# A two-layer decoder on one core: the order of all pieces on every engine set anew, in all five stages at once

## The reference, cut to what matters

```
x = x + bitnet_attention(ln(x), w_q, w_k, w_v, w_o)   # 16 heads of 16, causal; ternary weights, 8-bit activations
x = x + wkv(w, u, k=ln(x), v=ctx)                      # a recurrence over the 128 tokens, per channel
x = x + bitlinear(sigmoid(x1) * x2, w3)                # x1, x2 = bitlinear(ln(x), w1 / w2), ternary, width 704
x = x + attention(rope(q), rope(k), v) @ Wo            # 32 heads of 8 channels, 8 key heads, no mask
x = x + attend(q, [ssm_k, k], [ssm_v, v]) @ Wo         # q of [ctx, ln(x)]; keys of ctx in a window of 64,
                                                       # of ln(x) in one of 32; causal, with ALiBi
x = x + ln(x) @ W_base + b + shared low rank + top 2 of 6 low-rank experts
```

## Time and profile before

| what | us |
|---|---|
| median of three runs | 776.13 |
| lowest, highest | 775.43, 779.71 |
| the profiled execution, its whole time | 773.48 |
| its span in the trace | 771.7 |

### The profile page before, as it was taken

The page is one execution under the profiler, slowest core; times in us unless marked ns, Lnnn a source line. Parts: engine busy times, 40 slices in busy tenths (PEclk is TensorE's granted clock), DMA queues, the critical chain, the costliest instruction groups (busy, mean ns, idle before and its releaser), DMA issues. The chain is left out here.

```text
span 771.7 us, 19045 instructions
## 1 busy us (share of the span) xinstructions
PE 645.9 (84%) x6669; PEld 359.8 (47%) x6692; DVE 572.1 (74%) x1632; ACT 507.1 (66%) x1229; POOL 297.1 (39%) x472
## 2 busy tenths in 40 slices
PE   1598998865668779889999986799999999998885
...
DVE  5588886679999997678778754567676666666786
ACT  3588888587768766468887763366666766665421
...
GB/s 161 141 163 125 162 176 67 60 35 58 36 44 37 35 21 35 36 90 83 73 71 77 84 34 91 61 56 87 68 56 88 69 72 79 53 46 11 35 28 42
DMA packets 162303, 54.90 MB, mean 71 GB/s; under 512 B 148448, under 2 KB 160160, under 8 KB 161952
## 3 DMA queue, kind: packets, MB, share of 16 engines
...
## 5 line engine op out<-in xcount | busy, mean ns | idle before, releaser
L1163 DVE TENSOR_REDUCE l1x_neg_max<-bank 128x2 f16<-128x448 f32 (+1 forms) x192 | 119.6, 641 | 47.6 <-PE bank L1270 44.8
L1218 ACT ACTIVATE l1x_probs<-bank 128x512 f32<-128x512 f32 x192 | 106.4, 595 | 54.6 <-PE bank L1291 40.5
L871 DVE TENSOR_REDUCE l1a_neg_max<-bank 128x4 f16<-128x512 f32 x128 | 83.5, 684 | 32.7 <-PE bank L959 32.0
L1115 POOL TENSOR_TENSOR q_stack<-l1x_q_sum,q_stack 128x512 f16<-128x512 f32 x16 | 18.5, 1157 | 183.8 <-ACT q_stack L1210 183.8
L919 ACT ACTIVATE l1a_probs<-bank 128x512 f32<-128x512 f32 x128 | 69.5, 595 | 27.6 <-PE bank L973 27.0
L1662 PE MATMUL bank<-mix_xT_parts,w_ternary 128*128 128x256 f16 x384 | 50.0, 283 | 6.1 <-DVE mix_hidden L1544 4.0
L558 DVE TENSOR_REDUCE l_neg_max<-bank 128x4 f16<-128x512 f32 x64 | 42.3, 683 | 13.6 <-PE bank L685 13.6
L1662 PEld LDWEIGHTS bank<-mix_xT_parts,w_ternary 128*128 128x128 f16 x384 | 37.8, 102 | 15.3 <-DVE mix_hidden L1544 6.4
L1475 POOL TENSOR_TENSOR mix_hidden_parts<-mix_hidden,mix_hidden_parts 128x256 f16<-128x256 f32 x48 | 38.0, 804 | 15.1 <-ACT mix_hidden_parts L1607 15.1
L631 ACT ACTIVATE l_probs<-bank 128x512 f32<-128x512 f32 x64 | 36.6, 599 | 10.7 <-PE bank L705 10.7
L1734 POOL TENSOR_TENSOR moe_rstd<-moe_var_eps,minus_half 128x1 f32<-128x1 f32 x16 | 8.8, 550 | 75.2 <-DVE moe_var_eps L1752 75.2
...
## 6 DMA issues: line engine op xcount, KB each, us to landing
...
```

The lines of the kernel that those rows point to most:

```text
L871: dve.tensor_reduce(mm[:, 16 * j + 4 * s:16 * j + 4 * s + 4], b_s[c % 3][:].rearrange("p (r k) -> p r k", k=P), AX.X, ALU.max, negate=True ...
L1163: dve.tensor_reduce(mm[:, first:first + count], scores, AX.X, ALU.max, negate=True).then_inc(s_max, 1)
L1218: act.activation(prob[:, c, :], b_st[c % 2][:], ACT.Exp).then_inc(s_exp, 1)
```

## The change

Every entry of `ORDERS`, `PACE` and `TIMES` is replaced, and `clock` takes four paces a stage, one for each quarter of its batches, in place of one. No instruction is added or removed, and no semaphore, buffer or piece is changed.

```diff
 ORDERS = {
     ("l0", "dve"): order("""
-        S.2 F1+4 T3b-3 S.3 F1b+4 T3c-3 F3b+3 F8b.0+2 F3c+3 T3s-3 F3d+3 F1c+4 F8b.1+2 F8s+3 T5-3 S.0+1 S.1+1 T1-2
-        T1b-2 T3-2"""),
+        F3d T3s-6 F8b.0-1 F8b.1-1 T5-6 F1+2 F8s S.0-2 T1-5 S.1-2 T1b-5 T3-5 F1b+2 T3b-5 T3c-5 S.2-2 S.3-2 F3b+1 F3c+1
+        F1c+2"""),
     ("l0", "act"): order("""
-        F5+2 OE-2 ST.2-1 ST.3-1 F3+3 F8a.0+2 F8a.1+2 T3d-3 M T3e-3 F3e+3 T4-3 ST.0 F3f+3 F8v+2 ST.1"""),
+        T4-6 F3f ST.0-3 ST.1-3 F5 F3+1 OE-4 ST.2-3 ST.3-3 T3d-5 T3e-5 F8a.0 F8a.1 M-2 F3e+1 F8v"""),
     ("l0", "pe"): order("""
-        T4-3 S.0+1 T5-3 F5+3 T1-2 ST.1 S.1+1 F7+3 PV M+1 ST.0+1"""),
+        T4-6 M-3 ST.0-3 T5-6 F5 S.0-2 T1-5 ST.1-3 S.1-2 F7 PV-3"""),
...
     ("l1a", "act"): order("""
-        ST.7-2 ST.0-1 ST.1-1 F5+3 F8a.0+2 F8a.1+2 ST.2-1 ST.3-1 OE.1-2 M T4-3 ST.4-1 ST.5-1 F8+3 OE.0-1 ST.6-1"""),
+        ST.5-5 OE.0-5 ST.6-5 ST.7-5 F5 ST.0-4 ST.1-4 F8a.0-1 OE.1-5 ST.2-4 F8a.1-1 ST.3-4 T4-6 M-3 F8 ST.4-4"""),
     ("l1a", "pe"): order("""
-        T1.0-3 S.2 ST.0-1 PV.1-2 T1.1-3 S.3 ST.1-1 F7+3 T4-3 M ST.2-1 PV.0-1 S.0+1 T5-3 ST.3-1 S.1+1 F5+4"""),
+        ST.0-4 PV.1-5 T1.1-6 S.3-3 ST.1-4 F7 T4-6 M-3 S.0-2 ST.2-4 PV.0-4 T5-6 ST.3-4 S.1-2 F5+1 T1.0-5 S.2-2"""),
     ("l1x", "sp"): order("""
-        G-2 X-1 M-3 V-3"""),
+        X V-2 M-2 G"""),
...
     ("l1x", "act"): order("""
-        ST.0-1 ST.1-1 V+1 OE.1-2 F5+2 ST.2-1 ST.3-1 F8a.0+2 ST.4-1 ST.5-1 T4-2 F8a.1+2 ST.6-1 M ST.7-1 ST.8-1
-        ST.9-1 OE.0-1 ST.10-1 ST.11-1"""),
+        V-1 OE.1-4 F5 ST.2-3 ST.3-3 F8a.0 ST.4-3 ST.5-3 T4-4 ST.6-3 ST.7-3 M-2 ST.8-3 ST.9-3 F8a.1 OE.0-3 ST.10-3
+        ST.11-3 ST.0-2 ST.1-2"""),
     ("l1x", "pe"): order("""
-        ST.0-1 PV.1-2 S.3 ST.1-1 F5+2 S.4 T1.1-2 F7+2 ST.2-1 S.5 T4-2 ST.3-1 M T5-2 S.0+1 ST.4-1 PV.0-1 S.1+1
-        ST.5-1 T1.0-1 S.2+1"""),
+        S.4-2 T1.1-4 F7 ST.2-3 S.5-2 T4-4 ST.3-3 T5-4 M-2 S.0-1 ST.4-3 PV.0-3 ST.5-3 S.1-1 T1.0-3 ST.0-2 S.2-1 PV.1-3
+        S.3-1 ST.1-2 F5+1"""),
...
     ("moe", "pe"): order("""
-        DOWN-1 LORA-2 TR UP-2"""),
+        DOWN-1 LORA-2 UP-2 TR+1"""),
 }
...
-PACE = {"l0": (0, 8, 8.0, 11.73), "mix": (150.0, 1.35, 15.88, 5.97), "l1a": (263.0, 1.53, 8.18, 15.58), "l1x": (441.5, 6.93, 13.05, 26.37), "moe": (677.0, 5.96, 4.55, 4)}
+PACE = {"l0": (0, 1.941, (6.473, 6.712, 10.692, 8.665), 10.545),
+        "mix": (141.42, 2.413, (19.619, 5.266, 26.628, 11.892), 4.987),
+        "l1a": (248.9, 2.09, (8.933, 5.156, 7.122, 10.398), 13.65),
+        "l1x": (411.09, 11.822, (16.158, 18.43, 8.739, 9.691), 24.684),
+        "moe": (648.04, 7.98, (4.321, 5.181, 2.717, 13.573), 5.015)}
...
-    start, fill, pace, drain = PACE[stage]
-    return start + fill * min(turn - 1, 0) + pace * min(max(turn - 1, 0), n - 1) + drain * max(turn - n, 0)
+    start, fill, paces, drain = PACE[stage]
+    part = (n - 1) / len(paces)
+    run = sum(pace * min(max(turn - 1 - k * part, 0), part) for k, pace in enumerate(paces))
+    return start + fill * min(turn - 1, 0) + run + drain * max(turn - n, 0)
```

More of the change, by code:

```diff
@@ L128 @@
     ("l1a", "pool"): order("""
-        R+2 Rb+2 F1c+4 V+1 F8b+2"""),
+        R-1 Rb-1 V-2 F1c+1 F8b-1"""),
     ("l1a", "dve"): order("""
-        F1c+3 S.2-1 S.3-1 T1.0-4 F1+4 T1b.0-4 S.4-1 S.5-1 T1.1-4 S.6-1 T1b.1-4 S.7-1 F3+3 F1b+4 S.0 S.1 T5-4"""),
+        S.2-3 F1c+1 T1.0-6 F1+2 T1b.0-6 S.3-3 S.4-3 S.5-3 T1.1-6 T1b.1-6 S.6-3 S.7-3 F3+1 S.0-2 F1b+2 S.1-2 T5-6"""),
     ("l1a", "act"): order("""
-        ST.7-2 ST.0-1 ST.1-1 F5+3 F8a.0+2 F8a.1+2 ST.2-1 ST.3-1 OE.1-2 M T4-3 ST.4-1 ST.5-1 F8+3 OE.0-1 ST.6-1"""),
+        ST.5-5 OE.0-5 ST.6-5 ST.7-5 F5 ST.0-4 ST.1-4 F8a.0-1 OE.1-5 ST.2-4 F8a.1-1 ST.3-4 T4-6 M-3 F8 ST.4-4"""),
@@ L134 @@
     ("l1a", "pe"): order("""
-        T1.0-3 S.2 ST.0-1 PV.1-2 T1.1-3 S.3 ST.1-1 F7+3 T4-3 M ST.2-1 PV.0-1 S.0+1 T5-3 ST.3-1 S.1+1 F5+4"""),
+        ST.0-4 PV.1-5 T1.1-6 S.3-3 ST.1-4 F7 T4-6 M-3 S.0-2 ST.2-4 PV.0-4 T5-6 ST.3-4 S.1-2 F5+1 T1.0-5 S.2-2"""),
     ("l1x", "sp"): order("""
-        G-2 X-1 M-3 V-3"""),
+        X V-2 M-2 G"""),
     ("l1x", "pool"): order("""
-        F8b+3 F1c+4"""),
+        F1c+1 F8b"""),
     ("l1x", "dve"): order("""
-        S.2 F1+3 S.3 S.4 F1b+3 T1.0-2 F3+2 S.5 S.6 T1b.0-2 S.7 S.8 T1.1-2 T1b.1-2 S.9 F8+2 S.10 S.11 F1c+3 T5-2
@@ L142 @@
-        S.0+1 S.1+1 F8b+2"""),
+        S.7-2 S.8-2 T1.1-4 T1b.1-4 S.9-2 F1+1 S.10-2 S.11-2 F1b+1 F1c+1 F8 T5-4 F3+1 S.0-1 F8b S.1-1 S.2-1 S.3-1
+        T1.0-3 S.4-1 S.5-1 T1b.0-3 S.6-1"""),
     ("l1x", "act"): order("""
-        ST.0-1 ST.1-1 V+1 OE.1-2 F5+2 ST.2-1 ST.3-1 F8a.0+2 ST.4-1 ST.5-1 T4-2 F8a.1+2 ST.6-1 M ST.7-1 ST.8-1
-        ST.9-1 OE.0-1 ST.10-1 ST.11-1"""),
+        V-1 OE.1-4 F5 ST.2-3 ST.3-3 F8a.0 ST.4-3 ST.5-3 T4-4 ST.6-3 ST.7-3 M-2 ST.8-3 ST.9-3 F8a.1 OE.0-3 ST.10-3
+        ST.11-3 ST.0-2 ST.1-2"""),
@@ L146 @@
     ("l1x", "pe"): order("""
-        ST.0-1 PV.1-2 S.3 ST.1-1 F5+2 S.4 T1.1-2 F7+2 ST.2-1 S.5 T4-2 ST.3-1 M T5-2 S.0+1 ST.4-1 PV.0-1 S.1+1
-        ST.5-1 T1.0-1 S.2+1"""),
+        S.4-2 T1.1-4 F7 ST.2-3 S.5-2 T4-4 ST.3-3 T5-4 M-2 S.0-1 ST.4-3 PV.0-3 ST.5-3 S.1-1 T1.0-3 ST.0-2 S.2-1 PV.1-3
+        S.3-1 ST.1-2 F5+1"""),
     ("moe", "sp"): order("""
-        UP-2"""),
+        UP-6"""),
     ("moe", "pool"): order("""
-        LNc+2"""),
+        LNc+4"""),
     ("moe", "dve"): order("""
-        GATEg-2 LORA-2 LNc+1 LN+2 LOGIT-1 LOGITb-1 XN+1 GATE-1 GATEb-1 UP-2 GATEc-1 GATEd-1 GATEe-1
@@ L155 @@
-        GATEf-1 LNb+2"""),
+        GATEg-2 LORA-2 LN+2 LOGIT-1 LOGITb-1 XN+1 GATE-1 GATEb-1 LNb+2 UP-2 GATEc-1 LNc+2 GATEd-1 GATEe-1 GATEf-1"""),
     ("moe", "act"): order("""
-        TR+1 LORA LOGIT+1"""),
+        LORA-2 LOGIT-1 TR"""),
     ("moe", "pe"): order("""
-        DOWN-1 LORA-2 TR UP-2"""),
+        DOWN-1 LORA-2 UP-2 TR+1"""),
 }
```

53 lines of the change are left out of this document (27 added, 26 removed), and 38 rows, old and new, of the table TIMES.

## The result

The changed kernel takes 751.0 us (median; 746.9 to 755.6) against 775.8 (774.0 to 779.7) in the same comparison: a ratio of 0.9675, interval 0.9608 to 0.9742. That is 25 us faster. Forecast were 771.8 us for the likeliest case, with a range from 756 to 788; the time lies 5 us under its lower end. The profiled execution of the changed kernel took 755.58, its slowest, with a span of 753.8; against the profiled execution before (span 771.7) its trace shows 17.9 of the 25 us.

What follows compares the result with a forecast made beforehand. PE was taken to lead in l0, l1a and l1x and DVE in mix, so only idle time could move. The terms −7 − 3 + 0 + 4 − 4 + 8.7 − 3 = −4.3 took the 776.13 median to 771.8 us, range 756 to 788.

Steps and rivals of the forecast that it cites:

- the likeliest case: Whole kernel: the stage and seam terms add to −4.3 us, giving 771.8 us; chance 0.38, own range 765 to 779.
- l1x, +8.7: l1x: PE's shorter cover between M and ST.0 leaves a stall, +0.66 us a batch for 13 batches; bounds 0 to +18.5.
- the need: l1x: from M to ST.0 the max rows need 0.53 + 4.94 = 5.47 us, against 4.63 us of cover.
- case B: Rival, whole kernel: landings are quick, no new stall, only the gains stay, −17 us, 759.1 us; chance 0.22.
- l1a into l1x, −4: Seam of l1a and l1x: S.0's 2.72 us wait for kT goes, plus 1.3 us of PE idle; 0 to −8.
- l0, −7: l0: PE's hole at F5 shrinks by 0.37 us a batch, −5.5, plus −1.5 in the first batches.
- l0 into mix −3: Seam of l0 and mix: mix's statistics start 12 DVE pieces, 4.7 us, earlier; two thirds kept, range 0 to −6.
- mix 0: mix: DVE is 96% busy with the same pieces in another local order, so no gain or loss, ±3 us.
- l1a, +4: l1a: S.0 moved behind M waits for kT with nothing running, 0.3 us for 13 rounds; −1.5 to +13.
- moe, −3: moe: TR one batch further ahead removes DVE's 10.1 us tail wait, a third stays gained; 0 to −6.
- the signs that I had named: Profile checks, including l0 at 7.5 to 7.6 us, l1x waits of 0.5 to 1.2; wrong if a seam moves over 10.
- A: Rival, whole kernel: DMA landings decide, stalls in l1x (+18.5) and l1a (+11), sum +12.5, 788.6 us; chance 0.22.

Runs made afterwards that it cites:

- e8: The changed kernel with the start times of l1x and moe 6 us later in the due times; ratio to before 0.9773, 758.2 us.
- g1: e3 with the start times of l1x and moe 3 us earlier in the due times; ratio to before 0.9801, 759.4 us.
- e3: The changed kernel with l1a's S.0 on PE again behind ST.2 and PV.0, not right behind M; ratio to before 0.9655, 747.8 us.
- e11: The changed kernel with only PE's order in l0 as before; ratio to before 0.9734, 754.0 us.
- e1: The changed kernel with l0's order on all engines as before; ratio to before 0.9863, 765.1 us.
- e9: The kernel before with l0's new local order alone, on all engines; ratio to before 1.0048, 777.5 us.
- f1: The kernel before with l0's new order and new due times; ratio to before 0.9946, 771.3 us.
- e2: The kernel before with mix and all after it 8.5 us earlier in the due times; ratio to before 1.0071, 779.5 us.
- f2: f1 with mix and all after it 8.5 us earlier in the due times; ratio to before 0.9931, 770.9 us.
- e7: The changed kernel with moe's local order on all engines as before; ratio to before 0.9678, 750.6 us.

## Why the prediction was wrong

The side of the likeliest case was right (faster), its size was not: 4 us were forecast, 25 came, outside the range. By the milestones the largest errors are the seam of l1a and l1x (−11 instead of −4), l1x (+3 instead of +8.7) and the end (−7 instead of −3); and 7 of the 25 us are not in the profiled execution, which was the changed kernel's slowest of four. By its own steps:

- **l1x, +8.7: wrong, by the need.** The structure was right and the cover nearly (4.44 us of work against 4.63; M to the first issue 0.53, as worked out). The need was not: 4.06 us from first issue to use instead of 4.94, and the stall is 0.15 instead of 0.84. The steady batches of l1x keep their pace of 14.2 us. From batch 0 to batch 13 the stage takes 183.7 to 190.1 us in the profiles with the new order of l1x and 183.0 to 187.0 in those with the old. I had named zero as the lower bound and given the case B, no new stall, 0.22. My working had flaws of its own: the row without a wait for the rows gives an upper limit of 606.24 − 601.00 = 5.24 us, not 5.06, since they may have landed while PE waited for ACT; 0.66 times 13 is 8.6; and the 4.94 that I took is 2.96 + 1.98, so the stall of 0.84 already had some 2.0 us behind the last issue in it. With 2.57 it would have been 1.43, and no gain of 7 us was to be had from 2.0. The runs show 1.1.
- **l1a into l1x, −4: too small.** 11 us in the milestones; 7 were lost by 6 us of shift in e8 and 11 by 3 us in g1. Of two waits I had counted one as gone, with 1.3 us more, and let the one for the max rows stand. In fact the place of l1x's pieces also goes with how l1a drains: its last output starts at 488.3 instead of 500.4, and with the start 3 us earlier, in g1, at 490.4 instead of e3's 477.5.
- **l0, −7: the place right, the size near, the working only in part.** The hole of 0.64 us at F5 closed wholly, and not by a bit over half: 7.6 instead of 8.2 us a batch. I had named 7.6 too, but counted from 7.9, an average with the stage's ends in it. S.0's new place, which I had set down as a cost of 0.86 us, is what keeps the hole from opening again at T1 (e11). And the 1.5 us of the first batches came (27.2 instead of 28.8 for the first reduction), but not by F3d's place: e1, with l0's old order at the new due times, has them too (27.4), and e9, with the new order at the old due times, has not (30.8). The fall of S.3 of batch 15 in f1 is 8.3 us. The step that failed is the next one: a gain in one stage was added to the sum at its full size. Passed on to the end it was worth 4 us in f1, and 12 to 14 within the whole change.
- **l0 into mix −3, and mix 0: wrong in the parts.** Beyond l0's own 9, 9 us appear at the seam and 8 go in mix; my −3 is by chance near their sum. As a step alone the earlier mix is a loss (e2) or nothing (f2). I had said that DVE's idle time is the cover for it; e2 shows l0's last reduction 10.6 us late, by the intruder, and the changed kernel shows the same: 156.3, where f1, with mix at its old start, has 145.6.
- **l1a, +4: right in the mechanism, and inside the bounds.** S.0 waits for kT with nothing running, 0.5 us a batch in the first profile. The size differs between profiles: l1a is 2.6 to 7.1 us longer, of which 2.1 have another cause, not found (e3).
- **moe, −3: right in sign, wrong in cause.** The end is 7 us shorter and TR's wait is gone, but e7 shows that TR's new place is not needed for it.

Of the signs that I had named, l0's 7.6 us, more rounds of S.0 with a wait for kT (8 instead of 5) and the end of DVE's wait for TR came; the wait of 0.5 to 1.2 us in l1x did not, mix began 17.7 us earlier instead of 10, and the seam of l1a and l1x moved by 11 us, where I had called over 10 at a seam a sign of being wrong.

Rival B came nearest, with −17 in its sum where the profiled executions differ by 17.9; it was held to be as likely as A. That the two numbers agree is luck: B has no loss in l1a, where there is one of 7 us, and −4 and −3 where −11 and −7 came. By the medians its 759.1 is 8 us too high. What all cases shared, and what the runs refute, is the sum itself. Seams and stages were priced one by one as though each gain or loss went to the end unchanged. Of single parts put into the kernel before, three lose 4 to 6 us, one gains 4, and the two halves give 15 of the 25 us. The Trainium skill, page "DMA: Bandwidth & Descriptors", section "Rules for kernel authors", speaks for issuing early and waiting late. PE's 4.59 us less 0.53 until the first issue leave 4.06, just what the rows need, so that the cost of which it warns appears chiefly in batches 0 to 2, with waits of 3.07, 1.69 and 0.88 us, and is 0.15 us in the steady ones; here the trace bears the rule out by a noticeable amount only where the stage fills.
